# Shared-key attention: GpSimd adds four key tiles' exponentials, TensorE sums them half as often

## The reference, cut to what matters

```python
nx = _rmsnorm(X, g1)
Q = (nx @ Wq.T).reshape(B, S, H, dk).transpose(0, 2, 1, 3)    # B=4, S=1024, H=4, dk=32
Kc = nx @ Wkc.T
Vc = nx @ Wvc.T
scores = jnp.einsum('bhsd,btd->bhst', Q, Kc) * scale
attn = jax.nn.softmax(scores, axis=-1)
out = jnp.einsum('bhst,btd->bhsd', attn, Vc)
out = out.transpose(0, 2, 1, 3).reshape(B, S, d) @ Wo.T
X = X + out
```

## Time and profile before

| what | before |
|---|---|
| median of 3 runs | 4993.7 us (4991.56 to 4997.28) |
| the profiled execution, its own time | 4986.23 us |
| its span in the profile | 4984.9 us |
| granted TensorE clock, mean over the span | 0.974 of full speed |
| the attention of the last block: first add to end of last add | 4500.2 to 4764.6 us, 264.4 us of the span |

### The profile page before, as it was taken

How to read it: one execution, slowest core, us unless ns; L and a number is a source line. 1 busy time by engine, 2 the same in 40 slices (tenths; PEclk the granted TensorE clock), 3 DMA queues, 4 the chain that set the end, 5 groups by cost and what they waited for, 6 DMA issues and landing times.

```text
span 4984.9 us, 149644 instructions
## 1 busy us (share of the span) xinstructions
PE 4650.8 (93%) x62728; PEld 3225.4 (65%) x62728; DVE 4323.5 (87%) x8627; ACT 3294.6 (66%) x6496; POOL 2931.2 (59%) x3105
## 2 busy tenths in 40 slices
PE   6999997999999999999999999999996999989988
PEld 3444444777777777777777777777775555555567
DVE  7989997999999999999999999999995777768666
ACT  4888884666666666666666666666663677756643
POOL 1330304878877887788778877887873222006654
PEclk7999998999999999999999999999997899989999
DMA  0000100000000000000000000000000000000000
GB/s 25 2 1 2 34 6 25 23 11 12 13 27 11 12 13 27 10 12 13 27 11 12 13 27 11 12 13 11 11 9 27 2 2 2 2 17 1 1 1 18
DMA packets 51765, 63.72 MB, mean 13 GB/s; under 512 B 12821, under 2 KB 41259, under 8 KB 50323
## 3 DMA queue, kind: packets, MB, share of 16 engines
q1 hardware_dynamic: 51090, 54.14, 3.6%
HBM read 25.17 MB, written 4.19 MB: 6 GB/s over the span
## 4 chain that ended last, share of the span: by engine, by line
PE 55%; DVE 25%; ACT 8%; issue 8%; POOL 2%; DMA 0%; SPq 0%; DVEq 0%; POOLq 0%; ACTq 0%
PE psum L582 7%; PE psum L1182 6%; PE psum L1244 6%; PE psum L551 5%; PE psum L1227 4%; PE psum L1259 4%; PE psum L1191 3%; DVE a_top L731 3%; PE psum L1299 3%; DVE b_cross L1498 3%; PE psum L568 2%; DVE b_stat L1537 2%; DVE x L1531 2%; DVE x L1494 2%; PE psum L546 1%
## 5 line engine op out<-in xcount | busy, mean ns | idle before, releaser
L1651 POOL TENSOR_TENSOR x<-x,b_cross 128x512 f32<-128x512 f32 x768 | 984.4, 1285 | 58.9 <-DVE b_cross L1498 58.9
L1657 POOL TENSOR_TENSOR x<-x,b_norm 128x512 f32<-128x512 f32 x768 | 788.2, 1046 | 199.3 <-ACT b_norm L1338 198.3
L1259 PE MATMUL psum<-b_w_vo,b_mixed 128*128 128x128 f32 x6144 | 779.9, 275 | 0.3 <-issue 0.3
L1259 PEld LDWEIGHTS psum<-b_w_vo,b_mixed 128*128 128x128 f32 x6144 | 754.2, 192 | 26.8 <-issue 0.4
L731 DVE TENSOR_REDUCE a_top<-psum 128x2 f32<-128x1024 f32 x512 | 603.9, 1218 | 63.6 <-PE psum L551 60.2
L665 ACT ACTIVATE a_prob<-psum 128x512 f32<-128x512 f32 x1024 | 543.6, 598 | 58.7 <-PE psum L568 45.0
L1664 POOL TENSOR_TENSOR x<-x,b_stat 128x512 f32<-128x512 f32 x384 | 397.6, 1049 | 310.6 <-DVE b_stat L1542 310.4
L1331 ACT ACTIVATE b_square<-psum 128x512 f32<-128x512 f32 x768 | 462.7, 602 | 143.0 <-PE psum L1182 120.5
L1380 ACT COPY b_mixed<-psum 128x512 f32<-128x512 f32 x768 | 439.7, 601 | 130.5 <-PE psum L1244 130.4
L1494 DVE TENSOR_TENSOR x<-psum,b_table 128x512 f32<-128x512 f32 x768 | 516.2, 672 | 11.1 <-ACT b_square L1331 10.4
L1498 DVE TENSOR_TENSOR b_cross<-psum,b_table 128x512 f32<-128x512 f32 x768 | 522.4, 680 | 0.0
(11 more groups left out here) (360 smaller groups left out, 10657.7 us busy)
## 6 DMA issues: line engine op xcount, KB each, us to landing
b_prev<-b_xs_x SPq DMA_DIRECT2D x24, 384.0 KB
ab<-in_L_ffn_Wqkv SPq DMA_DIRECT2D x6, 1024.0 KB, 5.1
b_shifted_x<-y SPq DMA_DIRECT2D x24, 224.0 KB
b_shifted_f<-y SPq DMA_DIRECT2D x48, 112.0 KB, 2.1
ab<-in_L_ffn_Wqkv SPq DMA_DIRECT2D x6, 512.0 KB, 6.1
ab<-in_L_ffn_Wo SPq DMA_DIRECT2D x6, 512.0 KB, 7.7
b_prev<-b_xs_x SPq DMA_DIRECT2D x24, 112.0 KB
x<-in_L_attn_x SPq DMA_DIRECT2D x4, 512.0 KB, 6.7
```

The lines of the kernel that those rows point to most:

```text
L1259: made = e.matmul(banks[n][:, 0:D], mixed[:, h, :], w_vo[l % 2][:, h, :], start=h == 0, stop=h == 2 * PAIRS - 1)
L1651: e.tensor_tensor(turned, turned, crossing, ALU.add).then_inc(sem["roped"], 1)
L1657: e.tensor_tensor(rh, rh, bcast(norm[i % 2][:, 1, HPC * c:HPC * (c + 1)], 2, LDIM), ALU.mult).then_inc(sem["scaled"], 1)
```

## The change

After the two adds of a group of four key tiles, GpSimd adds the second of the two results and the first, in place: a new step `join`, four of them (one for each head) for each `k` of 3 and 7. A join waits until the add just before it is done. TensorE's `sums` group is then done for `k` of 3 and 7 only, 12 slots behind the start of the tile instead of 10, and waits for the joins. Bank 7 is started at `k` of 3. The ring of `added` tiles stays at 8: an add that overwrites a joined tile waits for the sums, one that overwrites a tile that was only read by a join waits for that join. `finish`, `invert`, `divide` and `conclude` of a unit come two slots later, `take` does not. In all, 64 adds of 128x512 come to GpSimd's 128, and 16 of TensorE's 32 sums groups go. Line numbers of the changed kernel are some higher: add is L2125, join L2130, sums L1948, values L1939, second L1928, conclude L1954.

```diff
@@ -1750,14 +1750,16 @@
                 put(base + DHEADS * k + g, "second", u, k, g)
                 if k % 2:
                     put(base + DHEADS * k + g, "add", u, k, g)
+                if k % 4 == 3:
+                    put(base + DHEADS * k + g + 1, "join", u, k, g)
             put(base + DHEADS * (k + 1) - 1 + LAG, "values", u, k)
-            if k % 2:
-                put(base + DHEADS * (k + 2) - 1 + LAG, "sums", u, k)
+            if k % 4 == 3:
+                put(base + DHEADS * (k + 2) + 1 + LAG, "sums", u, k)
         put(base + SCORES + LAG, "take", u)
-        put(base + SCORES + LAG + 4, "finish", u)
-        put(base + SCORES + LAG + 6, "invert", u)
-        put(base + SCORES + LAG + 8, "divide", u)
-        put(base + SCORES + LAG + 10, "conclude", u)
+        put(base + SCORES + LAG + 6, "finish", u)
+        put(base + SCORES + LAG + 8, "invert", u)
+        put(base + SCORES + LAG + 10, "divide", u)
+        put(base + SCORES + LAG + 12, "conclude", u)
@@ -1940,10 +1942,10 @@
                 if kind == "sums":
                     k = step[2]
                     q.wait_ge(sem["copied"], i)
-                    q.wait_ge(sem["added"], number["add", i, k, DHEADS - 1])
+                    q.wait_ge(sem["joined"], number["join", i, k, DHEADS - 1])
                     for g in range(DHEADS):
                         p = added[(number["add", i, k, g] - 1) % ADDED]
-                        made = e.matmul(banks[7][ROWS * g:ROWS * (g + 1), :], chip.ones[:, 0:ROWS], p[:, :], start=k == 1,
+                        made = e.matmul(banks[7][ROWS * g:ROWS * (g + 1), :], chip.ones[:, 0:ROWS], p[:, :], start=k == 3,
                                         stop=k == TILES - 1, skip_group_check=True, tile_position=(0, ROWS * g))
                     made.then_inc(sem["summed"], 1)
@@ -2114,9 +2116,18 @@
                     if j >= ADDED:
-                        q.wait_ge(sem["summed"], number["sums", *adds[j - ADDED][1:3]])
+                        u, before, head = adds[j - ADDED][1:]
+                        if before % 4 == 3:
+                            q.wait_ge(sem["summed"], number["sums", u, before])
+                        else:
+                            q.wait_ge(sem["joined"], number["join", u, before + 2, head])
                     p = [prob[(number["second", i, tile, g] - 1) % POWERS][:, :] for tile in (k - 1, k)]
                     e.tensor_tensor(added[j % ADDED][:, :], *p, ALU.add).then_inc(sem["added"], 1)
+                if step[0] == "join":
+                    i, k, g = step[1:]
+                    here, there = (added[(number["add", i, tile, g] - 1) % ADDED][:, :] for tile in (k, k - 2))
+                    q.wait_ge(sem["added"], number["add", i, k, g])
+                    e.tensor_tensor(here, here, there, ALU.add).then_inc(sem["joined"], 1)
```

More of the change, by code:

```diff
@@ L1834, in shared_attention @@
     sem = dict(moe.sem, **chip.semaphores("d", "dma_weights cleared k_split q_split v_copied topped raised shifted valued "
-                                               "added summed taken copied inverted finished parted_high parted"))
+                                               "added joined summed taken copied inverted finished parted_high parted"))
     with ExitStack() as scope:
```

## The result

| what | before | after |
|---|---|---|
| median of 5 runs | 4993.7 us (4989.4 to 4997.3) | 5017.1 us (5005.1 to 5026.0) |
| ratio of the times, 95% interval | 1 | 1.0047 [1.0037, 1.0058] |
| the profiled execution: own time, span | 4986.2, 4984.9 us | 5016.7, 5015.4 us |
| first add to the end of the last add or join | 264.4 us | 288.6 us |

The change makes the kernel slower by 23 us; 14 were forecast, and the range held. The profiled executions differ by 30 us. Of these, 5.1 us stand before the first add (4500.23 against 4505.32 us), where nothing was changed. So I read the attention itself, not the whole span.

The account below looks back on a forecast made before the run. GpSimd was to replace TensorE as the bound in the last four units: -2 us for the first four units, +7.1 and +8.5 for the next two pairs, rounded to +14 on 4993.7, giving 5007.7 us; range 4996 to 5022.

Parts of the forecast that it names:

- What bounds the kernel: Last block's attention: TensorE sets the pace before; after, GpSimd becomes the bound in the last four units.
- GpSimd's price: 64 joins added to GpSimd's work in the attention, at 1.28 + 0.12 = 1.40 us each.
- the dependence: Each join waits for the instruction just before it on GpSimd: 0.12 us each, 7.7 us for 64.
- The last two stretches: Fifth and sixth units, then the last two: GpSimd becomes the bound, +7.1 and +8.5 us.
- The first stretch: First four units: GpSimd 141.0 us against TensorE 142.6, order decides; 146 to 147 us expected, -2 us.
- the prediction's own signs of being wrong: Among them: first four units over 150 us or under 143; GpSimd idling tens of us while the stretch is longer.
- the loop of the sums group: Each half unit, first four units: joins, sums group, seconds and exponentials wait in turn; 16.9 us each, eight are 135 us.
- the upper bound's late splits: First four units: two splits, each 4.5 us later behind eight instructions instead of four; +9, in all +25, 5019 us.
- TensorE's saving: Fewer sums groups in the attention: 1.4 us saved in a unit; 5.7, 2.9 and 2.9 us by stretch, 11.4 in all.
- The tail: Work after the attention's last join: claimed to be as today.
- Rival 3: VectorE in the attention held up by busier GpSimd: 5.6 to 11 us more, 5013 to 5019 us; chance 0.13.
- Rivals 1 and 2: Attention: first, TensorE stays the bound, 4982 us, chance 0.05; second, GpSimd bound with packed joins, 4997 to 5003, chance 0.22.

Follow-up runs that it names:

- experiment 5: Changed kernel with one group left unjoined in the two units before the splits, or in the first and third: 5012.8 or 5014.1 us.
- experiment 1: Changed kernel with each join adding only 16, or 256, of 512 columns: 4985.2 or 4992.9 us, ratios 0.9991 and 1.0004.
- (4): Changed kernel with the sums group (and finish to conclude) two slots earlier, or two later: 5036.8 or 5012.2 us, ratios 1.0093 and 1.0044.
- (6): Both kernels without VectorE's normalization of the second to fourth sequence but its last instruction: before 4978.1 us (0.9969), changed 5007.9 us (1.0025).
- join16: Changed kernel with each join adding only 16 of 512 columns: 4985.2 us, ratio 0.9991.
- moved: Kernel before with all sums groups, and finish to conclude, two slots later and no joins: 4991.5 us, ratio 1.0000.
- join256: Changed kernel with each join adding only 256 of 512 columns: 4992.9 us, ratio 1.0004.

## Why the prediction was right, and where it was not

**What bounds the kernel** was right: in the last four units GpSimd took over from TensorE, at 98% and 96% (97% were named as the sign), and TensorE waits for it. In the first four it has 87%, where 93% were named.

**GpSimd's price** was right within 3%: 83.1 + 4.9 us for 64 joins is 1.375 us each, 1.40 was forecast. From the start of an add to the start of its join it is 1.36 us (4567.78 to 4569.14), from a join to the next add 1.24, as between two packed adds. So the dependence costs 0.12 us, as forecast; the forecast was a little high because it put these 0.12 us on top of 1.28 instead of 1.24.

**The last two stretches** were right: +5.6 and +9.4 us, +7.1 and +8.5 forecast.

**The first stretch was the failing step:** "In the first stretch the two are level, and then order decides. ... So I expect 146 to 147 us, 2 us less than today, and put it at **-2 us**." It came out at +9.2 us, and two of the prediction's own signs of being wrong are met: the first four units take over 150 us, and GpSimd idles there for 21.0 us while the stretch is longer. I compared sums of work over four units, 141.0 us against 142.6, and let the loop of the sums group decide the rest, with the splits filling idle time. What the runs showed in its place is the upper bound's late splits: a split stands behind eight instructions instead of four, and the next unit's first add comes 4.2 and 5.5 us later behind its exponential; 4.5 us were estimated. Leaving out just these joins brings the adds back to where they were and returns 6.2 of the 9.2 us (experiment 5). That the whole came out at +9.2, next to the +9 of that bound, is in part luck: some 3 us of it stand in the first and third unit, which the bound did not have, and the splits' part is about 6.

The account that goes with it is that the rings let the engines run only 12 exponentials apart, so the balance must hold unit by unit. In a pair of units, one has 24 adds and joins behind the split's 7.2 us and GpSimd runs nearly without a gap; in the other it has slack and waits 4.6 and 3.6 us for exponentials. That slack cannot be spent in the unit before. One pair took 80.0 us instead of 75.1 (4505.3 to 4585.3), the other 77.5 instead of 73.2. Of the first pair's 4.9 us, 4.0 lie between the last group of adds and the first add behind the split. That the whole loss comes from the joins' length is shown (experiment 1), that the loop is not its cause as well (4), and so are the splits' delays and their return (5), in a run that also has 8 joins fewer. That the ring of `prob` is what ties the units together is argued from the idle gaps in the rows; no run had a longer ring or moved the split away from the joins. How much of the rest goes through VectorE stays open (6).

**TensorE's saving** was priced at 11.4 us; the 1.4 us of a unit make 11.2 for eight. The most that a run showed is 9.7 (join16), with a different split over the stretches (3.9, 4.1, 1.7 against 5.7, 2.9, 2.9). The reasoning behind it, that a lone sums group costs 0.15 us more than a paired one, holds for TensorE's busy time (4.8 us in `moved`); the time of that run is no longer than before.

**The tail** "after the last join is as today" was wrong by 1.8 us: from the end of the last add to the experts' first transposes it was 5.4 us (4764.6 to 4770.0), and is 7.1 us (4793.9 to 4801.0).

**Rival 3** had its mechanism but not its effect: VectorE's busy time grew by 19.4 us, more than the 6 to 11 that I had estimated. Leaving out the normalization took nothing off the loss, so most of that work is off the path. But TensorE waits 5.7 us more for VectorE in the first stretch, and no run tells what that costs. **Rivals 1 and 2** fell with the stretches; join256 shows that joins of 0.75 us would have made the change level.

## What to carry to other kernels

Before giving an engine more work, compare its sum with the present bound's over every stretch that is no longer than the rings let the engines drift apart, not over the whole phase: slack behind a burst does not pay for the burst. The price of more work on an engine with slack need not be a slope; here it had a knee: 33 us cost 7, the next 35 cost 27. And ask what a saving on the bound engine can be worth at all: here no run showed more than 10 us, while the work that bought it was 88 us. When you cut a phase into stretches, cut at an event that is not itself late: here more than half of a stretch's loss was the delay of the mark.

## What was not expected of the hardware

TensorE's granted clock fell inside the attention, to a mean of 0.99, 0.95 and 0.95 in the three stretches after, against 1.00 in each before; GpSimd is the bound in the last two, and what this cost is not shown. It fell again in the tail. While TensorE waited 7.2 us for the last joins and after, the profile shows these stretches of the kernel after:

```profile
4785.00:4795.00 10.00, 2.14 (x16) 0.39 (x16) 0.00 (x0) 1.14 (x2) 8.64 (x7) 0.80 0.00 0
4795.00:4801.00 6.00, 2.94 (x14) 1.79 (x9) 1.38 (x2) 1.23 (x2) 0.00 (x0) 0.50 0.00 0
```

and of the kernel before:

```profile
4764.60:4770.00 5.40, 2.23 (x16) 1.15 (x17) 1.38 (x2) 1.23 (x2) 0.04 (x1) 0.90 0.00 0
```

A granted clock of 0.50 is the lower of the two levels, 1.2 GHz. The last sums group took 1.94 us instead of 1.07, the output projection 2.08 instead of 1.17: together the 1.8 us of the longer tail. So here the wait for the last joins was paid for once more behind it.
